# A perceiver layer on one core: three experts' weights split in the self stage, four fills moved, and a wait for query stores moved

## What is computed

```
x = x + cross_attention(layernorm(x), ctx)   # 16 heads, 16 batches of 64 queries and 1024 keys
x = x + self_attention(layernorm(x))         # 32 heads, 4 key heads, causal, 64 rows per batch
x = x + moe(layernorm(x))                    # 16 experts, 4 per row, and one shared expert
# expert: silu(x @ g.T) * (x @ u.T) @ d.T, with 256 hidden numbers
# routing: sigmoid scores plus bias, best 2 of 4 groups, best 4 experts in them
```

## Time and profile before

| What | Before |
|---|---|
| Median of 3 runs (lowest, highest) | 1462.76 us (1459.79, 1463.19) |
| Profiled execution: time | 1460.57 us |
| Profiled execution: span | 1458.7 us |
| Mean granted clock of TensorE | 0.969 |

### The profile page before, as it was taken

One profiled execution on the slowest core, in us unless ns is written; L12 is line 12 of the kernel. 1 busy time (PEld: TensorE's weight loads), 2 busy tenths in 40 slices (PEclk: granted clock), 3 DMA queues, 4 the chain that ended last, 5 costly groups with the idle time before them and its releaser, 6 DMA issues. The chain is left out here.

```text
span 1458.7 us, 22813 instructions
## 1 busy us (share of the span) xinstructions
PE 1348.2 (92%) x7136; PEld 1107.0 (76%) x7136; DVE 792.5 (54%) x1387; ACT 729.3 (50%) x1736; POOL 549.7 (38%) x336
## 2 busy tenths in 40 slices
PE   5999799999999999999997999998899989999991
PEld 4777577878787878787875888887678768787781
DVE  4444466666666666656664444445388833432245
ACT  2444466565656555655554777777222223333330
POOL 2430233233231415151113333334034396228975
PEclk9999899999999999999998999999899999999996
DMA  5786422141415151513041333532643266546767
GB/s 197 257 271 207 166 102 102 62 170 50 180 43 187 43 187 43 187 43 115 1 173 63 106 109 109 165 115 95 233 153 121 80 223 202 177 129 215 249 193 223
DMA packets 78984, 209.66 MB, mean 144 GB/s; under 512 B 5888, under 2 KB 39168, under 8 KB 72960
## 3 DMA queue, kind: packets, MB, share of 16 engines
q1 hardware_dynamic: 69472, 163.65, 32.2%
q0 software_dynamic: 7136, 38.80, 7.9%
q10 hardware_dynamic: 2304, 6.29, 1.1%
HBM read 154.46 MB, written 92.01 MB: 169 GB/s over the span
## 5 line engine op out<-in xcount | busy, mean ns | idle before, releaser
L787 DVE TENSOR_TENSOR probsT_lo<-psTr,probsT_hi 128x512 fp32r<-128x512 f32 x256 | 176.6, 690 | 166.1 <-ACT probsT_hi L740 165.8
L740 ACT CAST probsT_hi<-psTr 128x512 fp32r<-128x512 f32 x256 | 150.2, 587 | 197.6 <-PE psTr L874 193.9
L874 PE MATMUL psTr<-ident,probs 128*128 128x128 f32 x1024 | 153.7, 274 | 12.0 <-DVE probsT_lo L787 5.9
L874 PEld LDWEIGHTS psTr<-ident,probs 128*128 128x128 f32 x1024 | 124.4, 141 | 51.6 <-DVE probsT_lo L787 14.6
L782 DVE TENSOR_REDUCE nmax<-psS 128x1 f32<-128x1024 f32 x128 | 155.3, 1214 | 14.0 <-DMA qe<-stage 7.3
L696 ACT ACTIVATE probs<-psS,nmax 128x1024 f32<-128x1024 f32 x128 | 143.8, 1123 | 14.9 <-DVE nmax L782 14.9
L652 POOL TENSOR_TENSOR w_slots<-ctx_f,w_slots 128x512 fp32r<-128x512 f32 x32 | 41.4, 1294 | 279.4 <-ACT w_slots L703 279.4
L79 PE MATMUL psS<-w_slots 128*128 128x512 f32 x256 | 113.5, 443 | 6.6 <-ACT probs L696 4.7
L79 PE MATMUL psV<-probsT_hi,w_slots 128*128 128x512 f32 x256 | 114.8, 448 | 0.7
L79 PE MATMUL bank<-w_slots,ao_first_hi 128*128 (+1 forms) x244 | 104.3, 427 | 5.8 <-POOL w_slots L1618 3.0
L81 PE MATMUL psS<-w_slots 128*128 128x512 f32 x256 | 103.0, 402 | 0.0
(11 more groups left out here) (300 smaller groups left out, 3275.1 us busy)
## 6 DMA issues: line engine op xcount, KB each, us to landing
w_ahead<-w_exp POOLq DMA_DIRECT2D x14, 1536.0 KB, 7.4
qe<-stage SPq DMA_DIRECT2D x16, 1024.0 KB, 6.8
w_slots<-qe SPq DMA_DIRECT2D x15, 1024.0 KB, 4.9
wraw<-w_pairs SPq DMA_DIRECT2D x8, 1792.0 KB, 11.3
early<-xs SPq DMA_DIRECT2D x47, 256.0 KB, 2.8
xs<-h_rows SPq DMA_DIRECT2D x47, 256.0 KB, 2.1
early<-ctx SPq DMA_DIRECT2D x16, 512.0 KB, 9.7
ao<-attn_out SPq DMA_DIRECT2D x32, 256.0 KB, 2.9
```

What stands on the lines that cost most here:

```text
L740: act.copy(PT[k % PTN].hi[:], psT[slot][:]).then_inc(turned_hi, 1)
L787: dve.tensor_tensor(out, psT[slot][:], f32(hi), ALU.subtract).then_inc(turned_free, 1)
L874: last = pe.transpose(psT[slot][:, q * P:(q + 1) * P], src(q), ident[:])
```

## The change

1. Cross: VectorE's wait for the query stores moves behind the four maxes, and ScalarE gets the same wait behind the four exps.
2. Fills: none in the first iteration, three in each of six; none in the self stage.
3. Self: the raw weights of experts 7, 10 and 13 are loaded in three pieces each (128x1024), split by GpSimd and stored, high and low, to the new DRAM array `w_pre`. The loads of w_o move to the last iteration, into partly other buffers. The semaphores of the cross stage are cleared and used again.
4. MoE: for experts 7, 10, 13 (WHOLE) GpSimd loads both parts into the slot by two DMAs. They are told ready (`w_ready`) behind the split of the next expert. The table then holds, for an expert, the number reached when it and all before it are ready (READY). Raw loads run over the twelve others (SPLIT).
5. Three small tiles of the table's computation lie in `gate_f` instead of buffers of their own.

```diff
+FILLS = 3
@@ build_cross, SP
         def iteration(i, first, last):
+            if not (first or last):
+                fill(FILLS * i - FILLS)
             if not last:
-                fill(2 * i)
                 for j in range(2):
                     load_kv(2 * i + 2 + j)
             for j in range(2):
...
                     sp.dma_start(XT[:], x_d[i]).then_inc(xt_in, 16)
-            if not last:
-                fill(2 * i + 1)
+                if not (first or last):
+                    fill(FILLS * i - FILLS + 1 + j)
@@ build_cross, ScalarE
         for rt in range(RT):
             exps(0, 0, rt)
+        act.wait_ge(stage_out, 32 * (NP + 1))
@@ build_cross, VectorE
-        dve.wait_ge(stage_out, 32 * (NP + 1))
         for rt in range(RT):
             maxes(0, 0, rt)
+        dve.wait_ge(stage_out, 32 * (NP + 1))
@@ build_self
-WO_STEPS = (2, 4, 6, 7)
+WO_STEPS = (0, 1, 2, 3)
+PIECES, PIECE = 3, KC * BANK // 2
+PRE_FIRST, PRE_STEP, NPRE = 7, 3, NT // 2 - 1
...
+    def has_group(v, last):
+        return not last and v >= HKV
+
+    def has_before(i, v):
+        return v < HKV and not (isinstance(i, int) and i == 0)
@@ build_self, SP
+        for done in keep["cleared_later"]:
+            sp.sem_clear(done)
         def step(i, v, last):
             u, tt, g, ahead = plan(i, v, last)
-            if isinstance(u, int) and u in WO_STEPS:
-                c = WO_STEPS.index(u)
-                if c == 0:
-                    sp.wait_ge(w_ready, WCH)
+            pre_moves(i, v, last)
+            if last and v in WO_STEPS:
+                c = WO_STEPS.index(v)
+                if c:
+                    sp.wait_ge(p_out[c - 1], 32 * NPRE)
                 sp.dma_start(wo_raw[c], t["w_o"][:, c * KC:(c + 1) * KC, :]).then_inc(wo_in[c], 16)
...
-            if g == 2 and not last and not isinstance(i, int):
-                r = 2 * NT - 4 + 2 * i + v // HKV
-                sp.dma_start(t["xs_r"][r], t["zeros"]).then_inc(keep["fill_in"], 16)
+        def pre_moves(i, v, last):
+            g = v % HKV
+            if g < PIECES and has_before(i, v):
+                m = i - 1
+                sp.wait_ge(pre_lo, PIECES * m + g + 1)
+                for part, src in enumerate((p_high[g], p_raw[g])):
+                    sp.dma_start(t["w_pre"][m, part, g], src).then_inc(p_out[g], 16)
+            if g >= 1 and has_group(v, last):
...
+                sp.dma_start(p_raw[g - 1], t["w_exp"][PRE_STEP * m + PRE_FIRST + 1, :, (g - 1) * PIECE:g * PIECE]).then_inc(
+                    p_in[g - 1], 16)
@@ build_self, GpSimd
                 rope_q(u + 3, tt + (g + 3) // HKV, (g + 3) % HKV)
+            if g == 3 and has_group(v, last):
+                pre_low(i, 0)
+            if g < 2 and has_before(i, v):
+                pre_low(i - 1, g + 1)
             if ahead(1):
                 norm(u + 1, (v + 1) % 2)
+            if g >= 2 and has_group(v, last):
+                pre_high(i, g - 2)
+            if g == 0 and has_before(i, v):
+                pre_high(i - 1, 2)
...
+        def pre_high(m, j):
+            pool.wait_ge(p_in[j], 16 * m + 16)
+            pool.sem_inc(pre_seen, 1)
+            pool.tensor_copy(p_high[j].bitcast(F32R), p_raw[j]).then_inc(pre_hi, 1)
+
+        def pre_low(m, j):
+            pool.wait_ge(pre_hi, PIECES * m + j + 1)
+            pool.tensor_tensor(p_raw[j].bitcast(F32R), p_raw[j], p_high[j], ALU.subtract).then_inc(pre_lo, 1)
@@ build_moe
+WHOLE = tuple(PRE_FIRST + PRE_STEP * m for m in range(NPRE))
+SPLIT = tuple(e for e in range(1, NE) if e not in WHOLE)
+ORDER = sorted(range(NE), key=lambda e: e + 1.5 * (e in WHOLE))
+READY = [max(ORDER.index(a) for a in range(e + 1)) for e in range(NE)]
...
-    real = (np.arange(NE) < NE - 1).astype(np.float32)
+    real = np.append(np.diff(READY), 0).astype(np.float32)
@@ build_moe, GpSimd
+        def expert_load(j):
+            pool.wait_ge(w_ready, ORDER.index(SPLIT[j - 2]) + 1 if j >= 2 else 1)
+            pool.dma_start(raw[j % 2], t["w_exp"][SPLIT[j] + 1]).then_inc(pool_in[j % 2], 16)
+
+        def whole_load(e):
+            for part in range(2):
+                pool.dma_start(f32(slot(e)[part]).rearrange("p (s c) -> p s c", s=PIECES),
+                               t["w_pre"][WHOLE.index(e), part].rearrange("s p c -> p s c")).then_inc(whole_in, 16)
+
+        def whole_ready(e):
+            pool.wait_ge(w_ready, ORDER.index(e))
+            pool.wait_ge(whole_in, 32 * (WHOLE.index(e) + 1))
+            pool.sem_inc(w_ready, 1)
...
             pool.sem_inc(slot_free, 1)
-            pool.tensor_copy(slot(e)[0], raw[(e + 1) % 2]).then_inc(pool_hi, 1)
-            pool.wait_ge(pool_hi, e)
-            expert_low(e)
-            if e + 2 < NE:
-                expert_load(e + 2)
+            if e in WHOLE:
+                whole_load(e)
+                continue
+            pool.tensor_copy(slot(e)[0], raw[j % 2]).then_inc(pool_hi, 1)
+            pool.wait_ge(pool_hi, j + 1)
+            expert_low(e, j)
+            if e - 1 in WHOLE:
+                whole_ready(e - 1)
+            if j + 2 < len(SPLIT):
+                expert_load(j + 2)
```

More of the change, by code:

```diff
@@ L979, in build_self @@
     tab = sb("rope_s_tab", [P, 2, 3, DH // 2])
-    wo_raw = keep["ahead"] + [sb("wo_last", [P, KC, BANK])[:]]
+    wo_raw = [sb("wo_first", [P, KC, BANK])[:]] + keep["ahead"]
+    sets = [a.rearrange("p k x -> p (k x)") for a in keep["ahead"]]
+    p_raw, p_high = ([a[:, j * PIECE:(j + 1) * PIECE] for a in sets] for j in range(2))
+    p_in, p_out = keep["pre_in"], keep["pre_out"]
+    pre_seen, pre_hi, pre_lo = sem("pre_seen"), sem("pre_hi"), sem("pre_lo")
     WO = [Shared(ws, c * WSZ, (KC, D)) for c in range(HQ // 2 // KC)]
@@ L1076, in step @@
                 store(u - 1, tt if g else tt - 1, (g - 1) % HKV, (v - 1) % 2)
-            if g == 2 and not last and not isinstance(i, int):
-                r = 2 * NT - 4 + 2 * i + v // HKV
-                sp.dma_start(t["xs_r"][r], t["zeros"]).then_inc(keep["fill_in"], 16)
+        def pre_moves(i, v, last):
[6 more added lines that the diff above has]
+            if g >= 1 and has_group(v, last):
+                m = i
+                if isinstance(i, int):
+                    if v == HKV + 1:
+                        sp.wait_ge(w_ready, WCH)
+                else:
+                    sp.wait_ge(p_out[g - 1], 32 * m)
+                sp.dma_start(p_raw[g - 1], t["w_exp"][PRE_STEP * m + PRE_FIRST + 1, :, (g - 1) * PIECE:g * PIECE]).then_inc(
+                    p_in[g - 1], 16)
         def store(u, tt, g, j):
@@ L1407 @@
 ON_WAY = 3
+WHOLE = tuple(PRE_FIRST + PRE_STEP * m for m in range(NPRE))
+SPLIT = tuple(e for e in range(1, NE) if e not in WHOLE)
+ORDER = sorted(range(NE), key=lambda e: e + 1.5 * (e in WHOLE))
+READY = [max(ORDER.index(a) for a in range(e + 1)) for e in range(NE)]
+assert WHOLE[-1] < NE - 1 and PIECES * PIECE == 2 * KC * I + NIT * D
 C_BIAS, C_TRI, C_TRIG, C_DIAG = 0, NE, NE + NE * NE, NE + NE * NE + NG * NG
@@ L1469, in build_moe @@
     cw = sb("choice_weight", [P, NT, TOPK])
-    full, cum, tabx = sb("tiles_of", [P, NE]), sb("tiles_to", [P, NE]), sb("table_cols", [P, 4])
+    full, cum, spare = (gate_f[:, j, :] for j in range(3))
+    tabx = sb("table_cols", [P, 4])
     pairs = cmp_e[:].rearrange("p i a j -> p (i a j)")[:, 0:NG * GS * GS].rearrange(
@@ L1615, in slot, with expert_low @@
             return WS[:, at:at + wcol], WS[:, at + wcol:at + 2 * wcol]
-        def expert_low(e):
-            pool.tensor_tensor(slot(e)[1], raw[(e + 1) % 2], f32(slot(e)[0]), ALU.subtract).then_inc(w_ready, 1)
-        def expert_load(e):
-            pool.wait_ge(w_ready, e - 1)
-            pool.dma_start(raw[(e + 1) % 2], t["w_exp"][e + 1]).then_inc(pool_in[e % 2], 16)
+        def expert_low(e, j):
+            pool.tensor_tensor(slot(e)[1], raw[j % 2], f32(slot(e)[0]), ALU.subtract).then_inc(w_ready, 1)
+        def expert_load(j):
[9 more added lines that the diff above has]
+            pool.sem_inc(w_ready, 1)
         pool.sem_inc(a_lo, 1)
@@ L1635, in _ @@
         pool.sem_inc(w_ready, 1)
-        expert_load(2)
+        expert_load(1)
         for e in range(1, NE):
@@ L1639, in _ @@
                 pool.wait_ge(table_made, 2)
-            if e == 1:
-                pool.wait_ge(raw_in[0], 32)
-            else:
-                pool.wait_ge(pool_in[e % 2], 16 * (e // 2))
+            if e in SPLIT:
+                j = SPLIT.index(e)
+                if j == 0:
+                    pool.wait_ge(raw_in[0], 32)
+                else:
+                    pool.wait_ge(pool_in[j % 2], 16 * ((j + 1) // 2))
+            if e == WHOLE[0]:
+                for j in range(PIECES):
+                    pool.wait_ge(keep["pre_out"][j], 32 * NPRE)
             if e == 1:
@@ L2181, in build, with sem_second @@
                 build_queries(nc, ctx, sem_first, t, keep)
+            keep["cleared_later"] = []
+            second_sems = ExitStack()
+            def sem_second(name):
```

(5 more changed lines are left out.)

24 lines of the change are left out of this document (12 added, 12 removed).

## The result

| | Before | After |
|---|---|---|
| Median, 20 runs each | 1461.67 us | 1454.53 us |
| Profiled execution: time (span) | 1460.57 us (1458.7) | 1452.82 us (1450.5) |
| Mean granted clock of TensorE | 0.969 | 0.974 |

The ratio of the times is 0.994, with a 95% interval of 0.9922 to 0.9958: faster by 7.1 us by the medians. Two of the changed kernel's 20 executions counted as slow, 1469.24 us and one of 2747.06 us that nothing here explains; the ratio leaves them out, and without them its median is 1453.87 us. In another session the same kernel had 1454.21 us against 1460.35, ratio 0.9958 (0.9942 to 0.9974).

What follows compares the result with a forecast made beforehand. TensorE was 92% busy, but the end was set by GpSimd, whose gathers stand behind all fifteen splits. Gains of 5.0 + 0 + 0 + 1.4 = 6.4 us off 1462.76 gave 1456.4 us, range 1449 to 1464.

Steps and rivals of the forecast that it cites:

- Part 1: Start of the cross stage: with the query-store wait moved, first transposes start 4.2 to 5.7 us earlier; 5.0 taken.
- my two cases: Cross stage start: TensorE runs the third and fourth score sets at 2.4 GHz, done at 158.1, or 1.2 GHz, 159.7.
- Part 2: Cross stage fills: the query load behind the new fill lands near 379, its user starts at 388.87; cost 0.
- Part 3: Self stage: GpSimd's nine subtractions and casts fit beside rope and norm; cost 0, bounds 0 and 9 us.
- a split that does not fit: Rival, self stage: the norm is late in nine turns by 1 us each, a loss of 2.6, 1465.4 us; chance 0.07.
- Turns of unchanged length: Self stage sign: the added split work on GpSimd leaves the length of each turn as before.
- Part 4: Last stage: 31 us of splits leave GpSimd, mostly becoming two DMA waits of some 8 us; gathers start 1.4 us earlier.
- Fast transfers: Rival, last stage: three transfers land in 16 us, not 20; gain 14.4 in all, time 1448.4; chance 0.20.
- Slow transfers: Rival, last stage: tiles and weights share DMA; no gain at 23.2 us of transfers, 1468.4 at 26; chance 0.14.

Runs made afterwards that it cites:

- the eleven traces with part 1 and the three without: All profiled traces of this study, by whether the query-store wait was moved: first scores to self stage 619.3 to 620.0 us with it, 625.2 to 626.1 without.
- the wait alone: The kernel before with only the query-store wait moved behind the maxes and added behind ScalarE's exps: 1456.25 us, ratio 0.997.
- the fills alone: The kernel before with only the fills moved (none in the first cross iteration, three in each of six, none in the self stage): 1460.91 us, ratio 0.9998.
- the five with it as the change has it: Traces of the changed kernel (two), of it with the query-store wait undone, with additions spaced, and with semaphore clears late: tile 38 193.3 to 196.9 us after tile 0.
- gaps: The changed kernel with each VectorE addition of a gathered tile waiting for the one before: 1454.26 us, ratio 0.9967; also added to two kernels with experts told later.
- the parts alone: The kernel before with only the query-store wait moved, 1456.25 us, ratio 0.997; the changed kernel with only that move undone, 1460.78 us, ratio 1.0004.
- the high part alone: The changed kernel loading only the high part of experts 7, 10 and 13, computed inexactly: 1444.74 us, ratio 0.991.
- rows of 12 KB: The changed kernel with `w_pre` laid out as one run of 3072 numbers per partition, not three of 1024: 1456.03 us, ratio 0.9971.
- experts told later: Four variants of the changed kernel: experts 10 and 13, or only 13, told ready two splits later, each without and with spaced additions: ratios 0.9964, 0.9951, 0.9966, 0.9952.
- the nineteen and the nine additions above: Unbroken VectorE additions without a long gather issue: nineteen in the changed kernel with 12 KB rows (ratio 0.9971), nine with only the high part loaded (0.991).

## Why the prediction was right, and where it was not

The forecast was 1456.4 us, 6.4 less than before; measured are 1454.5, 7.1 less (6.1 less in the other session).

**Part 1**, forecast 5.0 (4.2 to 5.7). The mechanism held step by step: third set released at 152.92, fourth at 155.19, no wait for the stores. The length fell by 5.8 us, the upper end, since TensorE ran both sets at 2.4 GHz (granted clock 1.00 from 152.9 to 156.9, 0.40 us for a matmul), the better of my two cases, and not at the clock of the earlier trace rows. I had taken the middle of the two. Alone it gave 4.4 us in the timed runs. The gain arrived whole, as the step said: the cross stage behind the first turn took 608.08 us, before 608.96, and the eleven traces with part 1 and the three without bear it out.

**Part 2**, forecast 0. Right. The fills take longer than the 10.9 us of the earlier trace rows when three stand in an iteration:

```profile
DMA to landing us min/median/max: 9.1/16.2/20.9
```

But 16 us and more are those of the second and third of a group, queued behind one another; the new one, ahead of the load of queries, landed in 9.1 to 9.9 us. What my working had wrong is the wait behind it. I had the load start when the fill had landed, 10.9 + 5 us. The load of queries of the earlier trace rows, issued 1.6 us behind the new fill, landed in 11.3 us (the changed kernel, window 357 to 357.7):

```profile
DMA to landing us min/median/max: 11.3/11.3/11.3
```

The six such loads took 10.6 to 11.3 us in place of 4.8 to 5.1, so a fill ahead costs a load 6 us, where I had 9 (379 in place of 370). The next queries are used 24.3 us behind that issue, so 13 us of cover were left, and not 4 to 10.

**Part 3**, forecast 0. Right. The subtraction fits between rope and norm as in the working; one turn, timeline of GpSimd:

```profile
848.15 1.29 POOL L1137 TENSOR_TENSOR q_rope<-q_terms 128x512 f32<-128x512 f32 x1
849.40 2.39 POOL L1181 TENSOR_TENSOR w_ahead<-w_ahead 128x1024 fp32r<-128x1024 f32 x1
852.38 1.04 POOL L1141 TENSOR_TENSOR sprobs<-sprobs,srinv 128x512 f32<-128x512 f32 x1 [0.60 <-DVE srinv L1292]
853.37 1.04 POOL L1177 CAST w_ahead<-w_ahead 128x1024 fp32r<-128x1024 f32 x1
```

0.60 us of room was left (0.5 forecast), and the norm still waited for VectorE, not for the split. It is so in all nine turns, with 0.39 to 0.61 us. The rival of a split that does not fit is refuted. "Turns of unchanged length" holds from the second turn on; the 1.2 us or more that most executions add ahead of it (above) was not in my sum, and no run here says what it is.

**Part 4**, forecast 1.4. The two waits were right in place and near in size, 6.75 and 6.42 us where 8 was said, since the three transfers had landed after 18.4 and 17.9 us and not 20. An estimate by the Trainium skill (DMA: Bandwidth & Descriptors, Anatomy of one DMA) would have the three follow in 13 us. Neither one raw load (5.6 us by that fit, at least 6.9 in the changed kernel) nor three agree; here the tiles' transfers ran beside them. I had TensorE wait 1.6 us at tile 36, for expert 12; it did not, and waited 2.73 us at tile 39, for expert 13.

Two things were left out of the sum, of opposite sign. The gathers did start earlier than said: from the first split of the last stage (1174.36 before, 1166.70 after) to the first gather it is 227.4, 228.4 and 229.8 us in the three traces without part 4 (before, the wait alone, the fills alone), and 223.0, 228.9, 225.3, 222.0 and 223.7 in the five with it as the change has it: 4.0 less on average, with a scatter larger than that. Counted from the copy of tile 0 the two groups don't overlap: 205.0 to 206.3 us without, 200.5 to 204.1 with it, 3.7 less on average. Then the 31 gathers take longer: 48.05, 46.22 and 46.42 us without it, 51.90, 48.56, 50.79 and 48.55 with it and without gaps: 3.0 more. Net 1.0, near the 1.4 forecast, but as the difference of two larger terms. The long issue is some 1.9 of the 3.0 (4.2 and 3.5 us beyond a usual 1.2, in two of the four); what the rest is was not tried.

So the end came out right partly by luck. The sum by measured lengths is 5.8 + 1.0 = 6.8, and 7.1 was timed. The timed runs of the parts alone, 4.4 and -0.5, come to less; their intervals (0.1 to 8.5 us and -3.9 to 2.8) allow it.

**The rivals.** Fast transfers: no, 18 us and not 16. That they would have been worth it the high part alone suggests, though it also takes bytes from the tiles' way: 16.8 us in all, where the fast case said 14.4. Slow transfers: the mechanism is real and mild here. In the changed kernel tiles fell behind in both bursts, ScalarE waited 3.32 us for an output buffer (1.1 to 2.9 in the other four of the five traces), and with rows of 12 KB it took back all that the weights had won. TensorE's waits for experts told later did the same by another way: in those four kernels the first gather waited 9.6 to 12 us for tile 38. My working had the gathers follow the last split by the 1.45 us of the earlier trace rows; in the five traces with part 4 as the change has it they follow by 1.45 to 2.19, so it held to within 0.7 us. The tiles were close all the same. Where the first gather did wait for tile 38, in six other traces, it started 4.3 us behind that tile's copy; in the five it is 5.3 to 7.4 us.

## What to carry to other kernels

When work is moved off an engine by loading its result, count the bytes against the window in which they must land, and ask whose transfers stand beside them: here 31 us of splits left, 13 us of waiting took their place, the first gather came 4 us sooner, and the end moved by 1 us, since the gathers then took 3 us more. When the waits were hidden as well, the tiles held the gathers. A wait that guards a buffer belongs in front of the first write of that buffer, on every engine that writes it; that one moved line gave most of the gain. And a gain at an end where the next chain stands close behind the first (here the tiles, 1 to 3 us behind the splits) is worth no more than the distance to it.

## What was not expected of the hardware

An issue of a gather by GpSimd, 0.95 to 1.5 us otherwise (once 1.82), took 3.9 to 5.4 us in four traces, each time while VectorE ran ten additions on end whose two tensor inputs both lie in SBUF (the on-chip memory of the engines); the DMA share fell to 0.18 meanwhile (window of the changed kernel, columns as above):

```profile
1426.00:1430.00 4.00, 0.00 (x0) 0.00 (x0) 3.17 (x5) 0.00 (x0) 3.99 (x1) 0.84 0.18 68
```

The kernel before has the same at another place, GpSimd beside VectorE:

```profile
1164.10 4.47 POOL L1610 DMA_INDIRECT xs<-h_rows,slot_int  x1 [0.30 <-issue]
```

```profile
1164.38 3.34 DVE L1942 TENSOR_TENSOR w_slots<-w_ahead,w_slots 128x3072 fp32r<-128x3072 f32 x1
```

Here too both inputs of the 3.34 us subtraction are in SBUF, and the scatter's issue ends 0.84 us after it. This one is regular: in each of the fourteen traces the last scatter whose issue overlaps that subtraction took 2.96 to 4.47 us and ended 0.83 or 0.84 us behind it. The long gathers end in the same way, 0.8 us behind the last of the ten additions. So an issue can stand until VectorE's unbroken work on two SBUF inputs is over. That it must is refuted by the nineteen and the nine additions above.

The Trainium skill (SBUF — State Buffer, Who interferes with whom) tells of this stall for VectorE's copies in their two-port modes, and says, as an inference, that an operation with two SBUF inputs does not hold up descriptor generation. The same section has such an operation contend with a GpSimd instruction that reads SBUF. An indirect DMA takes its row numbers from a tile in SBUF (`slot_int`, `slot_sorted_int`), so these traces may show the second and need not contradict the first; no run here tells the two apart.
